# A graph network kernel: the near case of its second edge layer, with fewer steps between its stages

## The reference, cut to what matters

```
h = relu(layernorm(x))
x_i, x_j = h[dst], h[src]
msgs = relu(concat(x_i, x_j) @ mW1 + mb1) @ mW2 + mb2     # 128 -> 128 -> 64
agg  = segment_sum(msgs, dst, num_segments=50000)
x    = x + relu(concat(h, agg) @ uW1 + ub1) @ uW2 + ub2
```

## Time and profile before

| | |
|---|---|
| time, median of 3 runs | 2421.32 us (2419.44 to 2427.26) |
| the profiled execution: its own time, its span | 2421.7 us, 2419.1 us |
| second edge layer, from its first load to its last add | 1645 to 2186 us of the span |
| busy over the whole span: TensorE, VectorE, ScalarE, GpSimd | 65%, 64%, 36%, 70% |
| mean granted TensorE clock over the span | 0.684 |

### The profile page before, as it was taken

The page is one execution under the profiler, slowest core; times in us unless marked ns, Lnnn a source line. Parts: engine busy times, 40 slices in busy tenths (PEclk is TensorE's granted clock), DMA queues, the critical chain, the costliest instruction groups (busy, mean ns, idle before and its releaser), DMA issues. The chain is left out here.

```text
span 2419.1 us, 57388 instructions
## 1 busy us (share of the span) xinstructions
PE 1563.3 (65%) x16004; PEld 1340.3 (55%) x16004; DVE 1546.1 (64%) x5636; ACT 864.6 (36%) x3093; POOL 1689.1 (70%) x1413
## 2 busy tenths in 40 slices
PE   4886755555455454554555540005999999997998
PEld 2555645545455454554554540005999999994454
DVE  5995655555545555555555551894999999994554
ACT  3773322222222222222222221562333333333665
POOL 2775888888888888888888885746777777751322
PEclk6996555555555555555555555557999999998999
DMA  3775544444444444444444422565555555424664
GB/s 99 251 247 172 114 81 84 75 83 82 76 85 80 78 84 74 85 83 75 85 75 83 84 35 15 181 219 150 125 125 124 126 124 126 123 70 119 187 188 145
DMA packets 342562, 273.11 MB, mean 113 GB/s; under 512 B 144834, under 2 KB 273514, under 8 KB 342484
## 3 DMA queue, kind: packets, MB, share of 16 engines
q1 hardware_dynamic: 259028, 233.22, 33.3%
q0 software_dynamic: 81536, 38.61, 15.1%
q10 hardware_dynamic: 1920, 0.37, 0.1%
HBM read 206.69 MB, written 65.34 MB: 112 GB/s over the span
## 5 line engine op out<-in xcount | busy, mean ns | idle before, releaser
L1111 POOL DMA_INDIRECT x<-e_sums,e_to x392 | 622.7, 1588 | 126.1 <-issue 118.6
L1346 PE MATMUL bank<-e_parts,e_same 128*128 128x64 bf16 x2940 | 172.8, 241 | 579.9 <-DVE e_parts L1205 579.9
L1298 PE MATMUL bank<-e_window,e_onehot 128*128 128x64 f32 x2352 | 525.3, 422 | 16.5 <-DMA e_window<-wh 16.5
L1298 PEld LDWEIGHTS bank<-e_window,e_onehot 128*128 128x128 f32 x2352 | 511.8, 332 | 16.9 <-issue 16.8
L1096 POOL DMA_INDIRECT e_ends<-wh,e_ids x392 | 419.1, 1069 | 132.7 <-issue 101.2
L1346 PEld LDWEIGHTS bank<-e_parts,e_same 128*128 128x128 bf16 x2940 | 159.4, 129 | 595.9 <-issue 595.9
L823 POOL DMA_INDIRECT e_near_source<-h,e_near_ids x392 | 394.9, 1007 | 129.0 <-issue 90.2
L1244 ACT ACTIVATE e_sq<-e_ends 128x64 f32<-128x64 f32 x784 | 188.7, 242 | 680.0 <-DMA e_ends<-wh,e_ids 679.9
L1169 DVE SCALAR_TENSOR_TENSOR e_prod<-e_ends 128x64 f32<-128x64 f32 x392 | 65.5, 222 | 363.4 <-DMA e_ends<-wh,e_ids 363.4
L933 PE MATMUL bank<-e_near_to_edge,e_near_window 128*64 128x128 f32 x2352 | 154.5, 282 | 176.3 <-DMA e_near_window<-h 176.3
L933 PEld LDWEIGHTS bank<-e_near_to_edge,e_near_window 128*64 128x64 f32 x2352 | 130.8, 140 | 182.4 <-DVE e_near_to_edge L844 176.7
(11 more groups left out here) (150 smaller groups left out, 2857.7 us busy)
## 6 DMA issues: line engine op xcount, KB each, us to landing
e_window<-wh SPq DMA_DIRECT2D x392, 96.0 KB
e_near_window<-h SPq DMA_DIRECT2D x392, 96.0 KB
e_owners<-ends SPq DMA_DIRECT2D x98, 256.0 KB, 3.0
n_x<-x SPq DMA_DIRECT2D x98, 256.0 KB, 3.1
n_x<-in_x_dram SPq DMA_DIRECT2D x49, 256.0 KB, 2.8
wh<-n_wh SPq DMA_DIRECT2D x49, 256.0 KB, 2.0
x<-n_x SPq DMA_DIRECT2D x49, 256.0 KB, 2.3
e_rel<-rel SPq DMA_DIRECT2D x98, 128.0 KB, 3.3
```

What stands on the lines that cost most here:

```text
L1111: pool.indirect_dma_start(out=added_tab, out_offset=bass.IndirectOffsetOnAxis(ap=t.to[s][:, j:j + 1], axis=0), in_=t.sums[s][:, j, :], in_ ...
L1298: last = nc.tensor.matmul(bank[s % 2][:, j * D:(j + 1) * D], onehot, window, start=w == 0, stop=w == WK - 1)
L1346: last = nc.tensor.matmul(bank[6 + s % 2][:, i * D:(i + 1) * D], t.same[s][:, same_block(j, i), :], t.parts[s][:, part, j, :], start=j == ...
```

## The change

Only the three lists are changed. No instruction is added or removed, and no wait; the offsets and the order within a step are new.

```diff
@@ near_vector
-    rounds_of_blocks(dve, [(-10, place), (-10, of(add, 0)), (-8, bias), (-10, of(add, 1)), (-8, of(to_node, 0)),
-                           (-10, of(add, 2)), (-8, leave), (-10, of(add, 3)), (-8, of(to_node, 2)), (0, ids), (-8, low),
+    rounds_of_blocks(dve, [(-4, bias), (-5, place), (-4, of(to_node, 0)), (-4, leave), (-5, of(add, 0)), (-4, low),
+                           (-5, of(add, 1)), (-4, of(to_node, 2)), (-5, of(add, 2)), (-5, of(add, 3)), (0, ids),
                            (-2, of(to_edge, 0)), (-2, of(to_edge, 1)), (-2, of(to_edge, 2))], ESLOTS, GROUPS)
@@ near_scalar
-    rounds_of_blocks(act, [(-6, relu), (-8, high), (-4, copy_ends), (-8, mid)], ESLOTS, GROUPS)
+    rounds_of_blocks(act, [(-3, copy_ends), (-4, high), (-4, mid), (-3, relu)], ESLOTS, GROUPS)
@@ near_tensor
-    rounds_of_blocks(pe, [(-9, sums), (-3, find), (-3, turn), (-7, message), (-5, hidden)], ESLOTS, GROUPS)
+    rounds_of_blocks(pe, [(-3, find), (-3, turn), (-4, message), (-5, sums), (-3, hidden)], ESLOTS, GROUPS)
```

## The result

The changed kernel takes 2882.6 us (median of 4 runs, 2875.4 to 2891.6) where the kernel before takes 2423.7 beside it (4 runs, 2419.4 to 2427.3): a ratio of 1.189, 95% interval 1.186 to 1.192. The forecast was 2903. The profiled execution took 2878.8 us (span 2877.0), 457.1 more than that of before; the sum had said 482.

A forecast was written before the change was run, and what follows sets the result against it. TensorE was taken to bound the near stage before the change. The last add moves from 2186.4 to 1664 + 97 x 10.3 + 5.2 = 2668, 482 us more: 2904, for the median 2903; range 2725 to 2985.

The forecast's parts named there:

- the circle: Near stage: bias, VectorE's list, to_edge, find, turn, message, back to bias spans one step, 8.72 us at full clock.
- VectorE's part: VectorE's list in a near-stage step: from the start of bias to the last to_edge's end, 5.46 us.
- TensorE's load: find's first weight load stays behind the wait; if pulled ahead, the whole would be 5 us less.
- The clock: Near stage: the clock falls in most steps, about when find begins, for 3.5 us; adds 1.6 us a step.
- rival A: Near stage: the circle holds, the clock does not fall; step 8.72 us, time 2750 us; chance 21%.
- Rival B: Near stage: the circle holds, the clock stays at half; step 11.76 us, time 3047 us; chance 12%.
- the 1664: Start of the near stage: time in us on the trace's clock at which the first bias was expected.
- Hidden work: GpSimd, SyncE and ScalarE stand aside in a 10 us step; they would bound only one of about 5.1.
- Rival C: Near stage: step stays 5.25 us, gaining 12 us at the start, some 11 at the end; 2399 us; chance 3%.

The follow-up runs named there:

- e1b: Changed kernel with to_edge one group further ahead (offset -1 instead of -2), e1 again in another comparison: 2421.8 us beside 2426.0 for the kernel before, ratio 0.998.
- e3: Changed kernel with six unread matmuls behind hidden on TensorE, to fill its pause: 2987.4 us beside 2831.0 for the kernel before, ratio 1.055.
- e3b: The edit of e3 (six unread matmuls added to the changed kernel) in another comparison: 2988.9 us beside 2851.1 for the kernel before, ratio 1.050.
- e5: Changed kernel with place before bias and add 3 between to_edge 0 and 1, to_edge still at -2: 2916.0 us beside 2851.1, ratio 1.024.
- e6: Changed kernel with message ahead of find in TensorE's list: 2937.6 us beside 2851.1 for the kernel before, ratio 1.031.
- e2b: Changed kernel with place before bias, low behind to_node 2, to_edge at -1 among the adds; e2 again: 2420.8 us, ratio 0.997 to the kernel before.
- e4b: Changed kernel with sums moved from behind message to the head of TensorE's list: 3000.5 us beside 2851.1 for the kernel before, ratio 1.055.
- e1: Changed kernel with to_edge one group further ahead (offset -1 instead of -2): 2788.8 us beside 2831.0 for the kernel before, ratio 0.986.
- e2: Changed kernel with place before bias, low behind to_node 2, to_edge at -1 among the adds: 2841.5 us beside 2831.0 for the kernel before, ratio 1.000.

## Why the prediction was right, and by how much it was off

The step that decides held: the circle spans one step where it spanned two. e1b is the proof from the other side, one offset that makes it two again and returns 2421.8 us. The sum came as near as it did partly by luck: the circle at full clock was 0.1 us longer than summed (8.82), and the clock cost 0.12 less. The terms, with what the steady step of after measured:

| term (us) | forecast | measured |
|---|---|---|
| `bias` to `to_node` 0, with `place` | 0.55 | 0.69 |
| `bias` to `leave` | 1.11 | 1.22 |
| `bias` to `low` (its wait for `mid`) | 2.00 (0.22) | 2.11 (0.21) |
| `bias` to the last `to_edge`'s end | 5.46 | 5.54 |
| `to_edge` to `find` | 0.22 | 0.24 |
| `find` to `bias` at full clock | 3.04 | not seen whole; `find` to `message` 1.89 of 1.90 (e3) |
| what the clock adds | 1.6 | 1.48 (4.52 in all) |
| step | 10.3 | 10.30 here, 10.24 in the middle, 10.12 over all 97 |
| last `bias` to the last add's end | 5.2 | 6.4 |
| last add | 2668 | 2644.2 |

**VectorE's part.** Right to 0.1 us. `place` cost 0.69, at the upper bound of 0.7; the dependent adds and the new wait for `mid` came as summed; the wait of `leave` is gone.

**TensorE's load.** The load of `find` began 0.01 us ahead of its matmul, behind the same wait, again. The Trainium skill ("TensorE: Matmul & The Clock Gate", section on the array's detail, engine queue depths) has loads pulled ahead of matmuls in flight; here nothing is in flight when the wait ends, and this trace shows no gain from it.

**The clock.** The choice between A and the forecast rested on a single fall, in the earlier trace rows, and was the weakest step; it held: the granted clock falls about when `find` begins, stays at the lower level for some 3.4 us (2005.1 to 2008.5 in the step shown, 0.3 us of it ahead of `find`), and is back at full for VectorE's half. It does so in every step, where I had expected some to escape and some to fall twice. That e3b keeps 0.97 with the pause mostly filled, where e5 beside it has 0.84, shows the cause. Rival B is refuted by the stage's 0.83, rival A by 421 ns for the median matmul of `find`.

**The 25 us between 482 and 457.** Three terms. The step was 10.12 on average, not 10.3: 97 x 0.18 = 17.5 us less. A third of that is the steady step, which is 10.24; the rest is short steps at both ends (the last one, without a `find`, is 4.23), which I had counted as full ones. The first `bias` was 8 us earlier than the 1664 I had. 6 of them are the stage's own earlier begin, its first `find` being at 1644.61 and in before at 1650.7; the other 2 are the clock, which was back at full by the first `message` (1.10 us), where I had summed at half level. From the last `bias` to the end it was 1.2 us longer. Half of that is `sums`, which began 3.2 us behind `bias` and not 2.6, because it waits for the second `to_node`, where I had it start behind `low`; the other half is that the last two adds stand behind the first two. -17.5 - 8 + 1.2 = -24.3.

**Hidden work.** GpSimd, SyncE and ScalarE stood aside as said. What I had overlooked is the circle through ScalarE. It changed nothing here, being shorter, but C's condition "or `message` ahead of `find`" was not enough: e6 did exactly that, and VectorE's list then waited for `high` in nearly every step. (e6's time does not show it, since in its comparison the kernel before is not at 5.25 us a step either.)

**Rival C.** "Some 11 at the end" was wrong: e2b's steps and before's short last ones show that there is nothing to gain at the end. It did not enter the forecast, whose sum went by times on the clock of the trace.

## What to carry to other kernels

Before a hand-written pipeline is made shorter, write down for each pair of engines that feed each other how many steps one turn of the circle between them spans, counting every instruction that stands in the queue between the two. Where that span drops to one, the period is the sum of both engines' parts, whatever room each has, and the idle time can cost the clock as well (here some 3.5 us by the circle and 1.5 by the clock, on a step of 5.25). The one shortening here that kept both circles at two steps and reordered VectorE's list, e2b, was harmless and gained 0.3%: cut steps one producer at a time, and look for the second circle behind the first.

## What the runs showed of the hardware

**A pause in every step costs the clock in every step.** With pauses of about 3.5 us in a step of 10.24, the granted clock fell once in each step and came back each time, 0.83 to 0.84 in both runs of the changed kernel; with the pause filled but for 1.5 us or less it was 0.97, and with `sums` at the pause's end (e4b, the third comparison) 0.76. In e4b there were two waits in each step, 1.8 and 1.9 us on average, and none as long as 3.5.

**The falls are evenly spaced, and the steps follow.** The steady steps of the changed kernel repeat in fours (10.17, 10.30, 10.27 and 10.22 us) with a mean of 10.24. The falls of the clock are more even still: three in a row begin at 2005.08, 2015.32 and 2025.56, and of the 88 stretches at the lower level between 1700 and 2600 us 87 last 3.41 us and all but the first two begin 10.24 us after the one before (17.07 there); in the changed kernel run again all 88 do both. An estimate from these rows: a step of 8.8 us at full clock, of which a stretch of 3.41 us at half the clock costs up to 1.7, can be anything up to 10.5, and one that comes late against the fall has less of `find` in the stretch and is shorter for it. So the falls may hold the steps at 10.24. That is an inference; e5, which should have tested it, had late signals in it.

**The same kernel at two times.** The kernel before took 2419 to 2440 us in two comparisons and 2821 to 2871 in the two others. The traces of the latter show TensorE stopping about 0.5 us at a time within ready matmuls (192 times in 600 us in e1), and its signals reaching ScalarE and VectorE up to some 3 us late (2.36 and 3.37 in the rows of e3), in e3 and e3b as soon as the last stop within `sums` is over. I saw both only in the near stage. A late signal lengthens a circle, which would explain why the edits rank otherwise than in an undisturbed comparison: e1 gained 1.4% and e2 nothing. What brings this about was not found. The nearest rival is the chip: the long times are those of chips 3 and 11, the usual one that of chip 6 (for the first result no chip is on record), and the record has no chip with two comparisons, so what goes with the chip and what with the hour can't be told apart.
